# Making two of the three chunks of the second feed-forward product from split fp32r parts, split on ScalarE and GpSimd

## The reference, cut to what matters

```python
def ffn_layer(x, g, bln, W1, b1, W2, b2):
    mu = x.mean(-1, keepdims=True)
    var = ((x - mu) ** 2).mean(-1, keepdims=True)
    xn = (x - mu) / jnp.sqrt(var + 1e-05) * g + bln
    hg = xn @ W1 + b1                      # to 2 * 341 columns
    a, gate = jnp.split(hg, 2, -1)
    return a * jax.nn.gelu(gate, approximate=False) @ W2 + b2   # back to 128
for i in range(DEPTH):                     # 6 layers
    x = attn_layer(shift_tokens(x), Wqkv[i], q_scale[i], k_scale[i], Wo[i]) + x
    x = ffn_layer(shift_tokens(x), ln_g[i], ln_b[i], W1[i], b1[i], W2[i], b2[i]) + x
```

## Time and profile before

| What | Value |
|---|---|
| Median of 3 runs (lowest, highest) | 3935.38 us (3933.94, 3938.61) |
| Profiled execution, its own time | 3928.65 us |
| Its span | 3926.6 us |
| Mean granted TensorE clock | 0.986 of full speed |
| PE busy | 3690.6 us, 94% |
| VectorE busy | 3058.0 us, 78% |
| ScalarE busy | 2270.7 us, 58% |
| GpSimd busy | 2597.4 us, 66% |

### The profile page before, as it was taken

How to read it: one execution, slowest core, us unless ns; L and a number is a source line. 1 busy time by engine, 2 the same in 40 slices (tenths; PEclk the granted TensorE clock), 3 DMA queues, 4 the chain that set the end, 5 groups by cost and what they waited for, 6 DMA issues and landing times.

```text
span 3926.6 us, 163773 instructions
## 1 busy us (share of the span) xinstructions
PE 3690.6 (94%) x67712; PEld 2844.7 (72%) x67712; DVE 3058.0 (78%) x5829; ACT 2270.7 (58%) x4270; POOL 2597.4 (66%) x3029
## 2 busy tenths in 40 slices
PE   5999979999999999999999999999999999999998
PEld 3555557777767777677877678787677876777876
DVE  7666658888778888788887788887788887888876
ACT  3555546666546666456666366665466664566653
POOL 4545538787547887367887288775477873687870
PEclk8999989999999999999999999999999999999999
DMA  1000002222212222122222122222122221222220
GB/s 44 4 6 4 6 28 68 56 60 60 58 32 59 59 57 59 41 49 60 61 57 56 30 65 57 59 61 58 32 60 58 59 56 41 54 57 58 60 52 22
DMA packets 136313, 189.08 MB, mean 48 GB/s; under 512 B 38006, under 2 KB 58484, under 8 KB 135412
## 3 DMA queue, kind: packets, MB, share of 16 engines
q1 hardware_dynamic: 135540, 178.23, 17.7%
HBM read 22.67 MB, written 2.10 MB: 6 GB/s over the span
## 4 chain that ended last, share of the span: by engine, by line
PE 76%; issue 4%; DVE 2%; POOL 2%; ACT 0%; DMA 0%; POOLq 0%; SPq 0%; DVEq 0%; ACTq 0%
PE PS L1270 18%; PE PS L1417 10%; PE PS L1256 10%; PE PS L1294 8%; PE PS L1280 8%; PE PS L1258 8%; PE PS L1257 8%; PE PS L1476 2%; PE PS L1411 2%; PE PS L1454 1%; PE PS L1447 1%; POOL t L1182 1%; PE PS L1442 1%; POOL t L1187 0%; DVE m L1800 0%
## 5 line engine op out<-in xcount | busy, mean ns | idle before, releaser
L1182 POOL TENSOR_TENSOR t<-t 128x1024 f32<-128x1024 f32 x384 | 908.0, 2370 | 363.9 <-DVE t L1762 362.6
L1187 POOL TENSOR_TENSOR t<-t,rn 128x1024 f32<-128x1024 f32 x384 | 723.6, 1905 | 29.8 <-POOL rn L150 27.3
L1542 ACT ACTIVATE va<-PS 128x512 f32<-128x512 f32 x384 | 229.8, 599 | 614.4 <-PE PS L1258 611.6
L1760 DVE TENSOR_TENSOR t<-PS,rope 128x512 f32<-128x512 f32 x768 | 523.2, 681 | 26.1 <-ACT sq L1577 24.5
L1256 PE MATMUL PS<-w_hi,xh 128*128 128x512 f32 x1152 | 514.2, 446 | 22.3 <-DVE xl L1063 11.3
L1577 ACT ACTIVATE sq<-PS 128x512 f32<-128x512 f32 x768 | 454.1, 593 | 33.0 <-PE PS L1258 17.7
L1270 PE MATMUL PS<-constants,t 128*128 128x128 f32 x3072 | 443.8, 277 | 19.8 <-POOL t L1187 12.8
L1258 PE MATMUL PS<-w_lo,xh 128*128 128x512 f32 x1152 | 458.5, 398 | 0.0
L1257 PE MATMUL PS<-w_hi,xl 128*128 128x512 f32 x1152 | 457.5, 397 | 0.0
L1767 DVE TENSOR_REDUCE ss<-sq 128x16 f32<-128x1024 f32 x384 | 448.3, 1209 | 0.0
L1270 PEld LDWEIGHTS PS<-constants,t 128*128 128x128 f32 x3072 | 351.9, 141 | 68.9 <-POOL t L1187 15.9
(11 more groups left out here) (168 smaller groups left out, 7869.8 us busy)
## 6 DMA issues: line engine op xcount, KB each, us to landing
vs<-va SPq DMA_DIRECT2D x768, 130.0 KB
vs<-va SPq DMA_DIRECT2D x768, 65.0 KB
t<-in_L_ffn_Wqkv SPq DMA_DIRECT2D x18, 512.0 KB, 4.4
w_out<-in_L_ffn_Wo SPq DMA_DIRECT2D x6, 512.0 KB, 3.9
a_normed<-in_L_attn_x SPq DMA_DIRECT2D x8, 256.0 KB, 7.0
a_xo<-in_L_attn_x SPq DMA_DIRECT2D x8, 256.0 KB, 2.8
out<-total SPq DMA_DIRECT2D x8, 256.0 KB, 3.5
w_raw<-in_L_ffn_W SPq DMA_DIRECT2D x6, 341.0 KB
```

The lines of the kernel that those rows point to most:

```text
L1182: pool.tensor_tensor(mine[:, i, :], mine[:, i, :], t2[:, i, :], ALU.add).then_inc(done, 1)
L1187: pool.tensor_tensor(h, h, bc(rn[:, H * i:H * (i + 1)], 2, HB), ALU.mult).then_inc(done, 1)
L1760: dve.tensor_tensor(o1, src, bc(rope[:, 2 * i, t, :], 1, 8), ALU.mult)
```

## The change: diff and what it does

For chunks 0 and 1 (128 hidden columns each) `output` no longer multiplies in plain fp32. w2 is split once a layer into a high part (ScalarE copy to fp32r, slot (1, 3)) and a low part (POOL subtraction, slot (2, 3)). Each hidden chunk hT is split too: ScalarE copies it to hh (`high_hidden`, after the next chunk's gate), POOL subtracts to hl (`low_hidden`). `output` then runs three fp32r matmuls for each of the two chunks and the plain fp32 matmul for the third (85 columns). Before each of the two chunks it waits for that chunk's hl.

On POOL the eight subtractions of a pair's chunks stand between the older work, and that work is partly moved: the three weight thirds, formerly all in step 1, are now spread over steps 1 and 2, and in step 3 one `low_hidden` stands between the adds of k and q.

To make room, `on` now lies over pw, w1_raw over gel, and `zeros` shrinks to one column; the exponentials wait for `ot_mm` in place of `pt_mm`.

```diff
+        w2_hi, w2_lo = sb("w2_hi", [P, SPLIT, D], F32R), sb("w2_lo", [P, SPLIT, D], F32R)
+        hh, hl = sb("hh", [P, 2, SPLIT, N], F32R), sb("hl", [P, 2, SPLIT, N], F32R)
-        on = sb("on", [P, PAIRS, 2, HB])
+        on = pw
+        w1_raw = gel[:].rearrange("p a n -> p (a n)")[:, 0:2 * FF]
...
-            def rope_and_scale(lay, s, t):
+            def rope_and_scale(lay, s, t, between=None):
...
                 add(1, rk_made, addk_made)
+                if between is not None:
+                    between()
                 add(0, rq_made, addq_made)
...
+            def low_hidden(lay, i, a, j):
+                U = lay * B + i * 2 + a
+                pool.wait_ge(hh_made, SPLIT * U + j + 1)
+                pool.tensor_tensor(hl[:, a, j, :], hT[:, a, j, :], hh[:, a, j, :].bitcast(F32), ALU.subtract).then_inc(hl_made, 1)
+
+            def low_third(lay, n):
+                pool.wait_ge(hi_made, 3 * lay + n + 1)
+                i = THIRDS[n]
+                pool.tensor_tensor(w_lo[:, third(i)], w_raw[:, third(i)], w_hi[:, third(i)].bitcast(F32),
+                                   ALU.subtract).then_inc(lo_made, 1)
...
+                        pool.wait_ge(hi2_made, lay + 1)
+                        pool.tensor_tensor(w2_lo[:], w2[:, 0:SPLIT, :], w2_hi[:].bitcast(F32), ALU.subtract).then_inc(lo2_made, 1)
+                    if list(ages) == LAST:
+                        for j in range(SPLIT):
+                            low_hidden(lay, 0, 0, j)
...
                 def step(old, new):
+                    if old:
+                        low_hidden(lay, old, 0, 0)
                     if new is not None:
                         norm(new)
+                    if old:
+                        low_hidden(lay, old, 0, 1)
+                    low_hidden(lay, old, 1, 0)
                     if follows and old == 0:
                         scale_rope(lay + 1)
                     if follows and old == 1:
                         last_projected(pool, lay + 1)
-                        for n, i in enumerate(THIRDS):
-                            pool.wait_ge(hi_made, 3 * (lay + 1) + n + 1)
-                            pool.tensor_tensor(w_lo[:, third(i)], w_raw[:, third(i)], w_hi[:, third(i)].bitcast(F32),
-                                               ALU.subtract).then_inc(lo_made, 1)
+                        low_third(lay + 1, 0)
+                    if follows and old == 2:
+                        low_third(lay + 1, 2)
+                    if follows and new is None:
+                        rope_and_scale(lay + 1, 0, 0, lambda: low_hidden(lay, old, 1, 1))
+                    else:
+                        low_hidden(lay, old, 1, 1)
+                    if follows and old == 1:
+                        low_third(lay + 1, 1)
                     if follows and old == 2:
                         split_rest(pool, lay + 1, 0, 0)
-                    if follows and old == 3:
-                        rope_and_scale(lay + 1, 0, 0)
...
             def output(lay, i, a):
                 U = lay * B + i * 2 + a
                 pe.wait_ge(ffn_done, U + B - 1)
+                pe.wait_ge(lo2_made, lay + 1)
+                for j in range(SPLIT):
+                    pe.wait_ge(hl_made, SPLIT * U + j + 1)
+                    pe.matmul(PS[:, a, :], w2_hi[:, j, :], hh[:, a, j, :], start=(j == 0), stop=False)
+                    pe.matmul(PS[:, a, :], w2_lo[:, j, :], hh[:, a, j, :], start=False, stop=False)
+                    pe.matmul(PS[:, a, :], w2_hi[:, j, :], hl[:, a, j, :], start=False, stop=False)
                 pe.wait_ge(h_made, 3 * U + 5)
-                for j, (o, w) in enumerate(FC):
-                    last = pe.matmul(PS[:, a, :], w2[0:w, j, :], hT[0:w, a, j, :], start=(j == 0), stop=(j == 2))
-                last.then_inc(y2_mm, 1)
+                w = FC[SPLIT][1]
+                pe.matmul(PS[:, a, :], w2[0:w, SPLIT, :], hT[0:w, a, SPLIT, :], start=False, stop=True).then_inc(y2_mm, 1)
...
-                    act.wait_ge(pt_mm, at(T, 3, 2, c + 1))
+                    act.wait_ge(ot_mm, at(T, 3, 2, c + 1))
...
                     if ending:
                         gate(lay, 0, 0, 1)
+                        high_hidden(lay, 0, 0, 0)
                         gate(lay, 0, 0, 2)
+                        high_hidden(lay, 0, 0, 1)
...
+                    copy(w2_hi[:], w2[:, 0:SPLIT, :]).then_inc(hi2_made, 1)
...
+            def high_hidden(lay, i, a, j):
+                U = lay * B + i * 2 + a
+                act.wait_ge(h_made, 3 * U + j + 3)
+                copy(hh[:, a, j, :], hT[:, a, j, :]).then_inc(hh_made, 1)
...
                                 gate(lay, old, a, j)
+                                if j:
+                                    high_hidden(lay, old, a, j - 1)
```

More of the change, by code:

```diff
@@ L891, in windowed_layers @@
         VALUES = 3
+        SPLIT = 2
         w_hi, w_lo = sb("w_hi", [P, 3 * INNER], F32R), sb("w_lo", [P, 3 * INNER], F32R)
@@ L895, in windowed_layers @@
         rope = sb("rope", [P, 4, TPS, HB])
-        w1_raw = sb("w1_raw", [P, 2 * FF])
         w1_hi, w1_lo = sb("w1_hi", [P, 2 * FF], F32R), sb("w1_lo", [P, 2 * FF], F32R)
         w2 = sb("w2", [P, 3, D])
+        w2_hi, w2_lo = sb("w2_hi", [P, SPLIT, D], F32R), sb("w2_lo", [P, SPLIT, D], F32R)
         b1c = sb("b1c", [P, 2, 3])
@@ L924, in windowed_layers @@
         hT = shared[:].rearrange("p a (b n) -> p (a b) n", b=2).rearrange("p (a j) n -> p a j n", a=2)
+        hh, hl = sb("hh", [P, 2, SPLIT, N], F32R), sb("hl", [P, 2, SPLIT, N], F32R)
         rden = sb("rden", [P, 2, PAIRS])
-        on = sb("on", [P, PAIRS, 2, HB])
+        on = pw
         oT = sb("oT", [P, PAIRS, P])
         credit = sb("credit", [P, 48])
-        zeros = sb("zeros", [P, PAIRS, W])
+        zeros = sb("zeros", [P, 1])
         fsf = sb("fsf", [P, 2, N + 1])
@@ L964, in windowed_layers @@
         hi1_made, lo1_made = sem("hi1_made"), sem("lo1_made")
+        hi2_made, lo2_made = sem("hi2_made"), sem("lo2_made")
         xh_made, xl_made = sem("xh_made"), sem("xl_made")
@@ L995, in windowed_layers @@
         gel_made, h_made = sem("gel_made"), sem("h_made")
+        hh_made, hl_made = sem("hh_made"), sem("hl_made")
         y2_mm = sem("y2_mm")
@@ L1096, in load_ffn @@
             def load_ffn(lay):
-                sp.dma_start(w1_raw[:], W1[bass.ds(lay, 1), :, :].rearrange("a c n -> (a c) n")).then_inc(ffw_in, 16)
+                sp.dma_start(w1_raw, W1[bass.ds(lay, 1), :, :].rearrange("a c n -> (a c) n")).then_inc(ffw_in, 16)
                 for j, (o, w) in enumerate(FC):
@@ L1222, in slot @@
                         pool.wait_ge(hi1_made, lay + 1)
-                        pool.tensor_tensor(w1_lo[:], w1_raw[:], w1_hi[:].bitcast(F32), ALU.subtract).then_inc(lo1_made, 1)
+                        pool.tensor_tensor(w1_lo[:], w1_raw, w1_hi[:].bitcast(F32), ALU.subtract).then_inc(lo1_made, 1)
+                        pool.wait_ge(hi2_made, lay + 1)
[3 more added lines that the diff above has]
+                            low_hidden(lay, 0, 0, j)
                 attention(pool, lay, slot)
                 def step(old, new):
+                    if old:
+                        low_hidden(lay, old, 0, 0)
                     if new is not None:
                         norm(new)
+                    if old:
+                        low_hidden(lay, old, 0, 1)
+                    low_hidden(lay, old, 1, 0)
                     if follows and old == 0:
@@ L1669, in slot @@
                     act.wait_ge(ffw_in, FFW_IN * lay + FFW_IN)
-                    copy(w1_hi[:], w1_raw[:]).then_inc(hi1_made, 1)
+                    copy(w1_hi[:], w1_raw).then_inc(hi1_made, 1)
+                    copy(w2_hi[:], w2[:, 0:SPLIT, :]).then_inc(hi2_made, 1)
                 if (s, t) == (B - 1, 2):
@@ L1708, in _ @@
             act.wait_ge(made, 6)
-            copy(credit[:, 47:48], zeros[:, 0, 0:1]).then_inc(gel_made, 2)
+            copy(credit[:, 47:48], zeros[:]).then_inc(gel_made, 2)
             act.preload_act_table_set("natural_log_exp_and_others")
```

## The result

The changed kernel took **3987.16 us** in the median of four runs (3975.05 to 3991.45), beside 3935.26 for the kernel before (3933.94 to 3938.61): ratio 1.0126, 95% interval 1.01 to 1.0151. So it is slower, 4 us above the forecast of 3983 and inside the range. The profiled execution is the longest of the four, 3991.45 us with a span of 3989.6. The later comparisons had medians of 3931.37, 3951.27 and 3944.56 us for the same kernel before, so what follows compares ratios to before within one group of runs; 0.001 is 4 us. Such a ratio is not the quotient of the two medians and can lie up to 0.0015 beside it; where that matters, both are given. The changed kernel ran in the first group alone, so a difference of another run from it has an uncertainty of 10 to 15 us.

What follows compares the result with a forecast made beforehand. PE, 94% busy, sets the pace inside the stage, POOL at layer borders. Stalls of 9.7, rounded to 10 us a layer, times five, less 2.5 for the sixth: plus 47.5 on 3935.4, 3983 us; 8-in-10 range 3940 to 4004.

Steps and rivals of the forecast that it cites:

- PE's gain, 15 us: Each of 48 outputs on PE takes 2.26 us in place of 2.58, gaining 0.32, if no wait comes with it.
- pair 0: Step 0 of looped layers: four rope products delay POOL's last subtraction, plus 1.75, with VectorE's norm plus 3.4 us.
- pair 1: Step 1: a weight third delays the last subtraction, plus 0.3; fl, late through L1750 held by POOL, makes it 2.1 us.
- pair 2: Step 2: a weight third and L1746 stand before the last subtraction, so PE is done 1.9 us later.
- border: Step 3 to the next layer: add of k delays the last subtraction, add of q, half_ss and refinement: plus 2.3 us.
- taking turns: Pair 0: VectorE's L1746, L1748 and L1750 alternate with POOL's work and push POOL by 1.67 us.
- the shorter stall: Rival: L1750 unheld, POOL not pushed in pair 0, subtraction nearer 1.04; 5.8 us a layer, 3959 us; chance 0.22.
- longer attention slots: Sign of being wrong: attention slots that became longer or shorter, which nothing in the forecast foresees.
- L1750 held by POOL: Pair 1: VectorE's L1750, two SBUF inputs, waits for POOL's third and delays fl; 2.1 us held, 0.3 unheld.
- The clock: Rival: PE's new waits at pair ends lower its clock afterwards, adding some 20 us, 4003 us; chance 0.12.
- The faster case: Rival: subtractions end in time, PE keeps 15 us and pair 1's 1.5 us wait goes five times, 3913 us; chance 0.10.
- The wait ahead of `spread`: Pair 1: the 1.50 us wait caused by the thirds goes, since they no longer run beside L120.

Runs made afterwards that it cites:

- e3: Changed kernel with constant hh and hl, without hidden copies, subtractions and PE's waits for them, POOL's order as before: 3916.93 us beside 3931.37, ratio 0.9957.
- e4: Changed kernel with all copies and subtractions, but output in plain fp32 and PE waiting for subtractions only one pair later: 3965.24 us, ratio 1.0092.
- e7: Changed kernel with the first group of three matmuls in output(old, 1) made three more times in five looped layers, filling PE's waits: ratio 1.008.
- e9: Changed kernel with rope and add of k before the last two subtractions, thirds opening steps 1 to 3 after fl, state split in step 2: ratio 0.9931.
- e1: Changed kernel with all POOL's older work of each feed-forward step in front of both last subtractions: 3929.86 us beside 3931.37, ratio 0.9998.
- e11: Kernel before, without the change, with only the weight thirds and the state split moved as in e9: ratio 0.9981.
- e10: Changed kernel with only the thirds and state split placed as in e9; rope products and add of k stay between the last subtractions: ratio 1.0021.

## Why the prediction was right, step by step

**PE's gain, 15 us.** Right: 14.4 in e3 by the medians, 17 by the ratio. The sixth layer's -2.5 was -2.7.

**The new instructions.** ScalarE's copy 0.63: 0.622. POOL's subtraction 1.28: median 1.287, mean 1.322 with those that VectorE held. The w2 split, 0.4 on ScalarE and 0.7 on POOL a layer and costed at nothing, took 0.40 and 0.74; e3 agrees that it costs nothing.

**The steps of a layer.** The net shift against before that each step adds in the second layer, counted from ScalarE's table load to the second gate behind the pair (the first gate can still lie in the low stretch), at the border to the refinement. In a low stretch fp32r matmuls start 0.43 us apart in place of 0.23; what the stretch costs is an estimate from this spacing of the weight loads.

| | forecast | measured | of it clock | rest |
|---|---|---|---|---|
| pair 0 | 3.4 | 3.7 | 1.6 | 2.1 |
| pair 1 | 2.1 | 3.0 | 1.4 | 1.6 |
| pair 2 | 1.9 | 3.0 | 1.6 | 1.4 |
| border | 2.3 | 1.3 | 0 | 1.3 |
| sum | 9.7 | 11.0 | 4.6 | 6.4 |

The total came out close because sizes were wrong in opposite directions, and that is luck: the clock, 4.6 in this layer, was not in the sum, and the waits themselves were put 3.3 too high. In pair 0 the term "taking turns", 1.67, was too large: the rope products took 3.17 in place of 2.77 and the last subtraction 1.71 in place of 1.28, together 0.83; and the gate of chunk (1, 1) stood 0.7 ahead of before and not 0.32. In pair 1 the forecast's own times give 1.9 (1663.2 less 1661.27) and not 2.1. At the border half_ss was not held: in each of the five layers it took 0.18 us; in the second it ran at 1722.40, just ahead of the add of q at 1722.47, ScalarE made the seed from it during that add, and the refinement followed the add at once (1724.79). So the 0.18 + 0.60 that the forecast put behind the add fell away, most of the 1.0 that the border was put too high. Without the clock a layer costs 6.4, near the 5.8 of the shorter stall: L1750 was held all the same, but the pushing of POOL and the held half_ss were put too high.

**Outside these stages.** The forecast named longer attention slots as a sign of being wrong, and they came: 6.5 us behind the first refinements, and 3.5 ahead of the first changed stage. These 10 of the 63 us between the two profiled executions are in no term of the sum. With 28 us more at the low clock in the attention stages, the clock is the likely cause; no run tried it. Not all of it comes from the waits: e3, which has none of them, also has some 140 us of low clock in place of 110.

**L1750 held by POOL** was the step of which the forecast was least sure; it holds (2.73 in place of 0.69; 15 of its 48 instances are long, three a looped layer, none in the sixth), and e4 shows that VectorE's held `norm` moves pair 1 by itself. Held with it were L1746 and L1748, which the forecast's sum had at their own time (1.50 and 1.37 in place of 0.55 and 0.43). The Trainium skill, SBUF: State Buffer, "Who interferes with whom", has a VectorE instruction with two SBUF inputs contend with a GpSimd one that reads SBUF; the trace agrees, at 693 to 2739 ns.

**The clock** was the step that failed: put down as a rival of 0.12 and left out of the sum. It fell behind all three pairs of the second layer and lasted 10.2 us at the border, and by e7 it is worth 18 us (12 in the feed-forward stages of the profiled executions), near the rival's 20. The rival was described rightly and should have been a term, with the reserve that it fell behind 9 of the 15 pairs.

**The faster case**, with 0.6 us of slack if nothing stood between the last subtractions, forecast 3913, 22 under before. e9 makes that condition true and measures 27 under (21 by the medians), with no wait for a subtraction in the second layer. e1 shows what the case had overlooked: moved forward, the old work holds VectorE's small chain, and that makes the chunk late.

**The wait ahead of `spread`**, put at 1.5 a layer: gone in the changed kernel (L120 never over 173 ns), and worth 7 us by e11.

## What to carry to other kernels

Work for an idle engine is not priced by its busy share but by its place: 127 us of subtractions on an engine with a third of its time free cost 50 us in one order and let the kernel gain 27 in another, some 20 of them by the change itself. When one queue gets a new deadline, list what stands between its inputs and it, and then ask which instruction of a neighbour the displaced work will run beside: here each of the first two places for the thirds only traded one held chain for another. And where PE gets new waits like these (2.1 to 3.3 us in the second layer), give the low clock behind them a term in the sum; here it was about a third of the loss. Work for PE in the waits, as in e7, tells how much.

## What was not expected of the hardware

VectorE's instructions with one SBUF input were held as fully as fl: L1792 took up to 1504 ns for 546, the cast L1794 up to 1370 for 428, and in e1 L122, on 8 columns, 2.31 us for 0.17. The holding goes both ways: the last subtraction of pair 0 took 1.71, 1.28 alone, beside a held fl of 1.10. And waits of the same length differ in what they do to the clock: in the changed kernel it fell at the waits of pair 1 in the second and third layers and stayed at full speed in the other three, and so it did behind pair 2, with a single wait of 2.27; in e4 it fell behind a single one of 3.89 in four layers of five, and in e10 it stayed up behind the 3.3 of pair 0 in the first. What decides it, and why one attention stage had more low stretches than another, was not tried.
